# Cross attention of layer 0: the own scores' exponential one task later on ScalarE, every copy of turned rows in the own tasks by ScalarE, and the filling shared anew

## The chip, the cores and the metric

The kernel runs on one core of a Trainium2 chip. The metric is the device time of one execution in microseconds; lower is better. All arithmetic is in f32.

## The reference, cut to what matters

Two decoder layers run over `x` of shape (8, 112, 512): attention, cross attention and a feed-forward block each. The change lies in the cross attention of layer 0. It computes attention over the sequence's own rows and, beside it, attention over a context of 375 rows, with shared projections:

```python
q = split_heads(hidden_states @ Wq, q_len)           # 32 heads of 16
k = split_heads(hidden_states @ Wk, q_len)
v = split_heads(hidden_states @ Wv, q_len)
q = q * cos + _rotate_half(q) * sin
k = k * cos + _rotate_half(k) * sin
scores = jnp.einsum('bhqd,bhkd->bhqk', q, k) * inv_sqrt_d
scores = jnp.maximum(scores + attention_mask, jnp.finfo(scores.dtype).min)
w = jax.nn.softmax(scores.astype(jnp.float32), axis=-1)
attn_output = jnp.einsum('bhqk,bhkd->bhqd', w, v)
a_k = split_heads(adapter @ Wk, adapter_len)         # adapter: the context, 375 rows
a_v = split_heads(adapter @ Wv, adapter_len)
a_scores = jnp.einsum('bhqd,bhkd->bhqk', q, a_k) * inv_sqrt_d
a_scores = jnp.tanh(gate) * jax.nn.softmax(a_scores, axis=-1)
attn_output = attn_output + jnp.einsum('bhqk,bhkd->bhqd', a_scores, a_v)
return attn_output.transpose(0, 2, 1, 3).reshape(bsz, q_len, hid) @ Wo
```

## The kernel before

One list of steps, made by `build_order`, is walked by every engine; each engine issues its own part of each step and skips steps in which it has none. So the order on every queue is the order of that list, and engines wait for one another by semaphores alone.

In the cross attention of layer 0 (8 batches) the 32 heads of a batch are taken in 4 groups of 8 heads. Each group is three **tasks** (`TASKS`): `own` (the 8 heads' scores over the sequence, 112x896), then context task 0 and context task 1 (4 heads each, 112x375 a head). There are 96 tasks. All three kinds put their scores into PSUM banks 0 to 3, so the scores of one task wait until the task before has read them out. A task's later parts lie one to three tasks behind (`attendx`):

- task n, scores: `xs` (own, L1032) or `xc` (context, L1043) on TensorE.
- task n, own: VectorE adds the mask and so empties the banks (`xm` 0, L1420), takes the maximum (L1426), clamps it (L1432) and subtracts it (L1434). ScalarE then takes one exponential over 112x896 (`xe`, L1900), which sums of `xm` 3 (L1429) and the transposes of task n+2 read.
- task n, context: VectorE takes the maxima out of PSUM (`cm`, L1442, two heads each), ScalarE four exponentials out of PSUM with their sums (`ce`, L1908), which empty the banks.
- task n+2: the exponentials are turned by TensorE: `xt` (own, L1052, two banks) or `xct` (context, L1059, three banks, 12 transposes). Each turned bank is copied to SBUF as 112x448 or 125x448: `turned_by` gives the engine, ScalarE for 0 (L1915, L1921) and VectorE for 1 (L1449, L1455). Before the change the third of three `xct` banks is VectorE's.
- task n+3: products with the values, `xv` (L1069) and `xcv` (L1079), into bank 7; `xu` (L1927) copies it out on ScalarE.

So the own task of group c turns context task 0 of group c-1, context task 0 turns context task 1 of group c-1, and context task 1 turns the own scores of group c. Once per batch, `xd` (reciprocals, L1462, L1464), `xr` (L1087, L1932), `xb` (L1095, L1470 to L1475) and `xw` (the output projection, L1104, L1387) follow in the tasks 2 to 5 of the next batch.

The steps that take PSUM here beside the scores (`xct`, `xt`, `xb`, `xw` and all filling) share three banks, `LOW` = 4, 5, 6, in the order of the list (`place`).

Between a task's `head` (exponentials, maxima, transposes) and its `tail` (the value products) stands **filling**, work for later that needs no task: projections of the next batch's context (`ck`, L1011, copied by L1888 on ScalarE and L1404 on VectorE; `cv`, L1020, copied by L1895 and L1411), of its queries and keys (`pj`, L988; `rt`, L995), and `vx` (L1003). `cross` shares it out: a batch's whole cost times the task's share in `GAP` is a task's due, its own steps are taken off, and filling is laid in until the due is used up. Batch 7, the last, has no projection to fill with, only transposes for the experts (L908).

Of the kernel before, what the change touches and what calls it, by code (L numbers as in the profile page):

```python
# [176 lines left out]
def cost(step):  # L177
    return COST.get(step[0], 0.0)
# [60 lines left out]


TASKS = [(b, c, kind) for b in range(NBATCH) for c in range(4) for kind in ("own", 0, 1)]
GAP = {"own": 3.0, 0: 5.5, 1: 5.5}


def shifts(n):

    if n >= len(TASKS):
        return []
    b, c, kind = TASKS[n]
    return [("xm", b, c, k) for k in range(3)] if kind == "own" else [("cm", b, c, kind, r) for r in (0, 2)]  # L250


def attendx():

    gaps = []
    for n in range(len(TASKS) + 3):
        turns, tail, mine = [], [], shifts(n)
        if 2 <= n < len(TASKS) + 2:  # L260
            b, c, kind = TASKS[n - 2]
            turns = [("xt", b, c, par) for par in range(2)] if kind == "own" else [("xct", b, c, kind, t) for t in range(3)]
        head = []
        for k in range(3):
            head += mine[k:k + 1] + turns[k:k + 1]
        if n < len(TASKS):
            b, c, kind = TASKS[n]
            head += [("xe", b, c)] if kind == "own" else [("ce", b, c, kind, r) for r in (0, 2)]
        if 2 <= n < len(TASKS) + 2 and TASKS[n - 2][2] == "own":
            tail.append(("xm", *TASKS[n - 2][:2], 3))  # L270
        if n >= 3:
            b, c, kind = TASKS[n - 3]
            tail += [("xv", b, c, par) for par in range(2)] if kind == "own" else [("xcv", b, c, kind, t) for t in range(3)]
            if kind == 1:
                tail.append(("xu", b, c))
        gaps.append((head, tail))
    for b in range(NBATCH):
        for k, step in ((2, ("xd", b)), (3, ("xr", b)), (4, ("xb", b)), (5, ("xw", b))):
            head, tail = gaps[min(12 * (b + 1) + k, len(gaps) - 1)]
            if step[0] in ("xd", "xr") or 12 * (b + 1) + k >= len(gaps):  # L280
                tail.append(step)
            else:
                head.append(step)
            if step[0] == "xw":
                tail.append(("stats", 2, b))
    return gaps
# [10 lines left out]
def cross():  # L297

    out, gaps = [], attendx()
    for b in range(NBATCH):  # L300
        fill = context(b + 1) + [("load", "ct", b + 2)] * (b + 2 < NBATCH) + [("vx", b + 1)] if b + 1 < NBATCH else [("load", "front", j) for j in (1, 2, 0)]
# [9 lines left out]
        whole = sum(cost(s) for s in fill + late) + sum(cost(s) for n in mine for part in gaps[n] for s in part)  # L311
        unit = whole / sum(GAP[TASKS[n][2]] for n in mine)
        due = 0.0
        for n in mine:
            if n == mine[2]:
                fill += late
            out.append(("xs" if TASKS[n][2] == "own" else "xc", *TASKS[n][:2], *TASKS[n][2:][:TASKS[n][2] != "own"]))
            due += unit * GAP[TASKS[n][2]]
            head, tail = gaps[n]
# [193 lines left out]
def psum_use(step, late):  # L513
# [36 lines left out]
    if k in ("xt", "xct"):  # L550
        return LOW, 1, [(("even_out", "odd_out")[turned_by(step)], step)]
# [37 lines left out]
def turned_by(step):  # L589

    k, b, c, par = step[:4]
    return par if k == "xt" else int(step[4] == 2)


def chunk_starts(l):
# [29 lines left out]
def program(nc, a, out):  # L625
    with ExitStack() as ctx:
# [268 lines left out]
        def tensor(e, w):  # L895
# [166 lines left out]
            def xv(b, c, par):  # L1062
                if par == 0 and (b or c):
                    w.wait_ge(*at("ou", (b, c - 1) if c else (b - 1, 3)))
                w.wait_ge(*at("vx", (b,)))
                w.wait_ge(*out_of(("xt", b, c, par), turned_by(("xt", b, c, par))))
                for r in range(4):
                    h = (8 * c + 2 * r + par) * 32
                    o = e.matmul(PS[32 * r:32 * r + 32, 7, bcol(2 * (c % 2))], VX[b % 2][0:S, h:h + 32],  # L1069
                                 px_of["xt", b, c, par][0:S, bcol(r)], start=par == 0, stop=par == 1)  # L1070
                o.then_inc(*up("values", ("xv", b, c, par)))

            def xcv(b, c, par, t_):
                s = ("xct", b, c, par, t_)
                w.wait_ge(*out_of(s, turned_by(s)))
                w.wait_ge(*out_of(("cv", b, t_), t_))
                for r in range(4):
                    h = (8 * c + 2 * r + par) * 32
                    o = e.matmul(PS[32 * r:32 * r + 32, 7, bcol(2 * (c % 2) + 1)], Vc[b % 2][0:KC, t_, h:h + 32],  # L1079
                                 px_of[s][0:KC, bcol(r)], start=(par, t_) == (0, 0), stop=(par, t_) == (1, 2))  # L1080
                o.then_inc(*up("values", ("xcv", b, c, par, t_)))
# [1333 lines left out]
```

## Time and profile before

| | us |
|---|---|
| median of 3 runs | 1978.99 |
| lowest, highest | 1974.83, 1980.17 |
| the profiled execution, its own time | 1975.63 |
| its span, first to last instruction | 1973.7 |
| busy in the span: TensorE (PE) | 1848.8 (94%) |
| busy: VectorE (DVE) | 1027.8 (52%) |
| busy: ScalarE (ACT) | 591.2 (30%) |
| busy: GpSimd (POOL) | 392.7 (20%) |
| mean granted TensorE clock | 0.966 |

The busy share is a mean over stages. The tasks of the change run from 436 us, where the first `xs` starts, to about 1018 us, and the chain of work that ended last passes through TensorE for 74% of the whole span. The granted clock is a share of 2.4 GHz; 0.5 is 1.2 GHz.

### The profile page before, as it was taken

The page shows a single profiled execution, that of the slowest core. Times are in us where ns is not written, and L with a number is a line of the kernel's source. Part 1 is how long each engine was busy: PE and PEld are TensorE (multiplying, and loading weights), DVE is VectorE, ACT ScalarE, POOL GpSimd, SP SyncE. Part 2 cuts the span into 40 slices and gives each one's busy share as a digit, 9 for nine tenths or more (in the row PEclk, how much of TensorE's full clock was granted, in tenths as well). Part 3 has the DMA queues.
Part 4 walks back from the last instruction along what each step waited for, and adds up shares of the span by engine and source line. Part 5 has one row for each costly group of instructions (what it writes and reads, how often), then busy time and mean ns, then how long its engine had stood idle before and what let it go on. Part 6 is the DMA issues. An engine that isn't in the chain of part 4 may idle for free.

```text
span 1973.7 us, 29165 instructions
## 1 busy us (share of the span) xinstructions
PE 1848.8 (94%) x11802; PEld 1214.3 (62%) x11802; DVE 1027.8 (52%) x1892; ACT 591.2 (30%) x1899; POOL 392.7 (20%) x456
## 2 busy tenths in 40 slices
PE   6899999999999999999888999997899999999798
PEld 5766666645665665666554888876576674444344
DVE  3665556426566655566653111115644454464699
ACT  0223223315454444555640011100312213232411
POOL 2432222410110110110003000005121120000588
PEclk9999999999999999999888999998899999999899
DMA  9000002000000000000205888874000011543011
GB/s 377 21 1 1 1 1 102 1 30 17 1 17 16 2 17 1 17 17 2 108 27 225 303 334 333 341 270 142 1 1 1 1 72 77 224 166 117 0 38 38
DMA packets 30965, 170.70 MB, mean 86 GB/s; under 512 B 3848, under 2 KB 3848, under 8 KB 17168
## 3 DMA queue, kind: packets, MB, share of 16 engines
q1 hardware_dynamic: 28272, 161.50, 21.9%
q0 software_dynamic: 2560, 7.34, 1.2%
q8 instruction: 94, 1.54, 0.3%
q14 instruction: 39, 0.32, 0.1%
HBM read 155.98 MB, written 16.52 MB: 87 GB/s over the span
## 4 chain that ended last, share of the span: by engine, by line
PE 74%; DVE 12%; issue 4%; POOL 4%; ACT 3%; DMA 2%; SPq 0%; POOLq 0%; DVEq 0%; ACTq 0%
PE PS L1143 8%; PE PS L980 6%; PE PS L931 6%; PE PS L1223 6%; PE PS L1183 5%; PE PS L1020 5%; PE PS L1011 4%; PE PS L1152 4%; PE PS L1256 3%; PE PS L988 2%; PE PS L1043 2%; PE PS L1059 2%; PE PS L1079 2%; PE PS L1052 1%; PE PS L1214 1%
## 5 line engine op out<-in xcount | busy, mean ns | idle before, releaser
L2046 POOL TENSOR_TENSOR rstd<-veps,mhalf 112x1 f32<-112x1 f32 (+1 forms) x76 | 57.5, 758 | 623.3 <-DVE veps L1316 609.0
L1143 PEld LDWEIGHTS PS<-R,W 128*128 128x128 f32 x1344 | 155.9, 195 | 11.9 <-issue 11.9
L1442 DVE TENSOR_REDUCE nmx<-PS 112x2 f32<-112x750 f32 x128 | 114.0, 932 | 91.0 <-PE PS L1043 90.9
L1143 PE MATMUL PS<-R,W 128*128 128x128 f32 x1344 | 156.3, 278 | 2.2 <-DVE R L1613 2.2
L1908 ACT ACTIVATE R<-PS,nmx 112x375 f32<-112x375 f32 x256 | 142.8, 574 | 1.3 <-DVE nmx L1442 1.3
L1387 DVE TENSOR_TENSOR x<-x,PS 112x512 f32<-112x512 f32 x40 | 27.5, 687 | 194.6 <-PE PS L1223 90.5
L931 PE MATMUL PS<-xT,W 128*128 128x224 f32 x640 | 125.3, 356 | 0.0
L931 PEld LDWEIGHTS PS<-xT,W 128*128 128x128 f32 x640 | 122.3, 192 | 4.9 <-issue 4.4
L1059 PE MATMUL PS<-cst,R 112*125 112x112 f32 x768 | 107.8, 286 | 13.0 <-DVE R L1455 9.2
L1620 DVE TENSOR_TENSOR R<-R,PS 128x512 f32<-128x512 f32 x21 | 14.4, 687 | 201.9 <-PE PS L1143 201.9
L1256 PE MATMUL PS<-W 128*128 128x512 f32 x256 | 118.0, 604 | 0.0
L1059 PEld LDWEIGHTS PS<-cst,R 112*125 112x125 f32 x768 | 92.0, 191 | 37.8 <-issue 15.6
L1223 PE MATMUL PS<-W,R 128*112 128x512 f32 x256 | 113.2, 595 | 0.8 <-DVE R L1672 0.8
L980 PE MATMUL PS<-W,R 128*112 128x512 f32 x256 | 113.7, 597 | 0.0
L2064 POOL TENSOR_TENSOR R<-R 128x224 f32<-128x224 f32 x80 | 52.8, 660 | 271.4 <-DVE R L1337 271.4
L1287 PE MATMUL PS<-W,xT 128*128 128x512 f32 x224 | 102.4, 601 | 1.9 <-ACT xT L1849 1.9
L1860 ACT ACTIVATE R<-PS,small 112x112 f32<-112x112 f32 x256 | 87.0, 388 | 47.1 <-DVE small L1355 47.1
L1183 PEld LDWEIGHTS PS<-xT,W 128*128 128x128 f32 x512 | 96.9, 190 | 1.6 <-issue 1.6
L1183 PE MATMUL PS<-xT,W 128*128 128x224 f32 x512 | 97.5, 352 | 0.0
L1020 PE MATMUL PS<-W 128*125 128x512 f32 x192 | 92.4, 628 | 1.3 <-ACT W L1921 0.6
L1011 PE MATMUL PS<-W 128*128 128x375 f32 x256 | 87.0, 489 | 4.5 <-DMA W<-in_ctxT 3.9
L980 PEld LDWEIGHTS PS<-W,R 128*112 128x112 f32 x256 | 44.1, 177 | 67.6 <-issue 67.6
(292 smaller groups left out, 3310.9 us busy)
## 6 DMA issues: line engine op xcount, KB each, us to landing
W<-in_we SPq DMA_DIRECT2D x63, 1024.0 KB, 7.4
W<-in_entwT SPq DMA_DIRECT2D x8, 1024.0 KB, 7.0
W<-in_entpw SPq DMA_DIRECT2D x8, 1024.0 KB, 8.7
W<-in_ctxT SPq DMA_DIRECT2D x8, 750.0 KB, 4.2
R<-in_ctxT SPq DMA_DIRECT2D x8, 750.0 KB, 8.1
R<-in_ctx SPq DMA_DIRECT2D x8, 750.0 KB
xs_rows<-in_x SPq DMA_DIRECT2D x3, 1792.0 KB, 39.1
R<-xs_rows SPq DMA_DIRECT2D x21, 256.0 KB, 7.8
```

The source lines that it names most:

```text
L931: o = e.matmul(PS[:, m, ab * UT:(ab + 1) * UT], lw, xT[:, k, tok], start=k == 0, stop=k == 3)
L980: o = e.matmul(PS[0:S, m, :], OT[:, n % 2, c, :], Wo[:, g * 8 + c, :], start=c == 0, stop=c == 7)
L1011: o = e.matmul(PS[:, m, 0:SC], Wx[1][:, k, c * 128:(c + 1) * 128], CT[:, k, :], start=k == 0, stop=k == 3)
L1020: o = e.matmul(PS[0:KC, m, :], CT[:, k, t * KC:(t + 1) * KC], Wx[2][:, k, :], start=k == 0, stop=k == 3)
L1059: t = e.transpose(PS[0:KC, m, bcol(r)], p_of(b, c, par)[0:S, r, t_ * KC:(t_ + 1) * KC], ident[0:S, 0:S])
L1143: o = e.matmul(PS[:, m, c * 128:(c + 1) * 128], gate_up(j % 3, k, off + c * 128), BT[:, j % 2, k, :], start=k == 0, stop=k == 3)
L1183: o = e.matmul(PS[:, m, ab * UT:(ab + 1) * UT], Wlq[c // 2][:, c % 2, k, ab * 128:ab * 128 + 128], xT[:, k, tok], start=k == 0, stop=k == 3)
L1223: o = e.matmul(PS[0:S, m, :], LOT[:, n % 2, c, :], Wlo[2 * g + c // 4][:, c % 4, :], start=c == 0, stop=c == 7)
L1256: o = e.matmul(PS[:, m, :], W[:, wt, kk * D + m * 128:kk * D + (m + 1) * 128], W[:, pw, kk * D:(kk + 1) * D], start=k in starts, stop=k + ...
L1287: o = e.matmul(PS[:, m, :], xT[:, k, tcol(t)], wk[:, k, :], start=k == 0, stop=k == 3)
L1442: e.tensor_reduce(nmx[0:S, par, r:r + 2], PS[0:S, r:r + 2, 0:SC], AX.X, ALU.max, negate=True).then_inc(*up("cmax", (b, c, par, r)))
L1908: e.activation(p_of(b, c, par)[0:S, r, :], PS[0:S, r, 0:SC], ACT.Exp, bias=nmx[0:S, par, r:r + 1], accum_out=sums[0:S, b % 2, n:n + 1]).th ...
```

## The change

Three things, all in the order of the steps. `xe`, the exponential of the own scores, moves out of the own task into context task 0 behind it, where it stands behind the ScalarE copies of turned rows and ahead of the four `ce`. `turned_by` gives the third `xct` bank to VectorE only in context task 0 (`par` 1, third bank); in the own task (`par` 0) all three are now ScalarE's. And `GAP` gives context task 0 a share of 6.5 and context task 1 of 5.0, where both had 5.5.

```diff
-GAP = {"own": 3.0, 0: 5.5, 1: 5.5}
+GAP = {"own": 3.0, 0: 6.5, 1: 5.0}
...
         if n < len(TASKS):
             b, c, kind = TASKS[n]
-            head += [("xe", b, c)] if kind == "own" else [("ce", b, c, kind, r) for r in (0, 2)]
+            if kind == 0:
+                head.append(("xe", b, c))
+            head += [("ce", b, c, kind, r) for r in (0, 2)] if kind != "own" else []
...
 def turned_by(step):
     k, b, c, par = step[:4]
-    return par if k == "xt" else int(step[4] == 2)
+    return par if k == "xt" else int(step[3:] == (1, 2))
```

The lines of the program below the change lie two lower in the changed kernel: L1900 is L1902 there. No instruction is added or dropped; 32 copies of 125x448 change engine. Queues of GpSimd and of the DMA issues (SP) keep their order of instructions.

On ScalarE, batch 4, own task of group 1 and context task 0 behind it, before. L1921 are copies of turned rows, L1900 is `xe`, L1932 is `xr`'s copy, L1908 are `ce`, L1895 a copy of `cv`:

```order
L1927 ACTIVATE W<-PS 128x224
L1921 ACTIVATE row<-PS 125x448 x2
L1900 ACTIVATE R<-R 112x896
L1932 ACTIVATE rT<-PS 32x224
L1921 ACTIVATE R<-PS 125x448 x2
L1908 ACTIVATE R,sums<-PS,nmx 112x375 x4
L1895 ACTIVATE W<-PS 125x16x2x16
```

The same place now:

```order
L1929 ACTIVATE W<-PS 128x224
L1923 ACTIVATE row<-PS 125x448 x2
L1923 ACTIVATE R<-PS 125x448
L1934 ACTIVATE rT<-PS 32x224
L1923 ACTIVATE R<-PS 125x448 x2
L1902 ACTIVATE R<-R 112x896
L1910 ACTIVATE R,sums<-PS,nmx 112x375 x4
L1897 ACTIVATE W<-PS 125x16x2x16
```

The own task has a third copy, and the exponential of 112x896 stands behind the next task's two copies.

On VectorE, the same two tasks before. L1420 to L1434 are `xm`, L1455 the copies of turned rows, L1442 `cm`, L1470 `xb`:

```order
L1420 TENSOR_TENSOR R<-PS,R 112x896
L1426 TENSOR_REDUCE sx<-R 112x8
L1432 TENSOR_SCALAR sx<-sx 112x8
L1434 SCALAR_TENSOR_TENSOR R<-R,sx 112x896
L1455 COPY R<-PS 125x448
L1442 TENSOR_REDUCE nmx<-PS 112x2 x2
L1455 COPY W<-PS 125x448
L1470 TENSOR_TENSOR R<-W,PS 128x448
```

And now:

```order
L1422 TENSOR_TENSOR R<-PS,R 112x896
L1428 TENSOR_REDUCE sx<-R 112x8
L1434 TENSOR_SCALAR sx<-sx 112x8
L1436 SCALAR_TENSOR_TENSOR R<-R,sx 112x896
L1444 TENSOR_REDUCE nmx<-PS 112x2 x2
L1457 COPY W<-PS 125x448
L1472 TENSOR_TENSOR R<-W,PS 128x448
```

The first of the two copies is gone from between the own scores' subtraction and the next task's maxima.

On TensorE, batch 5, context task 0 of group 1 up to the own task of group 2, before (L1043 `xc`, L1059 `xct`, L1095 `xb`, L1079 `xcv`, L1052 `xt`, L1104 `xw`, L1032 `xs`, L1020 the filling `cv`):

```order
L1043 MATMUL PS<-W,R 112x375 x4
L1059 MATMUL PS<-cst,R 125x112 x12
L1095 MATMUL PS<-rT,cst 128x112 x8
L1079 MATMUL PS<-R,W 32x112 x12
...
L1104 MATMUL PS<-W,R 112x512 x4
...
L1032 MATMUL PS<-R 112x112 x8
L1059 MATMUL PS<-cst,R 125x112 x12
L1020 MATMUL PS<-W 125x512 x4
```

And now:

```order
L1045 MATMUL PS<-W,R 112x375 x4
L1061 MATMUL PS<-cst,R 125x112 x12
L1097 MATMUL PS<-rT,cst 128x112 x8
L1022 MATMUL PS<-W 125x512 x4
L1081 MATMUL PS<-R,W 32x112 x12
...
L1106 MATMUL PS<-W,R 112x512 x4
...
L1034 MATMUL PS<-R 112x112 x8
L1061 MATMUL PS<-cst,R 125x112 x12
```

One `cv` has moved from the own task into the context task 0 that had no filling but `xb`. In all, ten steps of filling move between neighbouring tasks: into context task 0 go `ck` of batches 2, 4 and 5 (first quarter) and `ck` 7 (last quarter), `cv` 6 and `vx` 6 from own tasks, `cv` 3, one `pj` and one `ck` 7 from context tasks 1, and one `rt`. Of batch 7, where there is nothing to move, all stands as before.

## Rows read from the trace of the kernel before

**Rows 1.** Windows: busy us (count) of PE, PEld, DVE, ACT, POOL, clock, DMA share, GB/s

```profile
425.00:1020.00 595.00, 563.13 (x5037) 363.07 (x5036) 365.13 (x518) 300.53 (x826) 54.63 (x74) 0.96 0.06 20
```

**Rows 2.** Waits of TensorE, 425 to 1020 us: total us, times, longest

```profile
PE PS L1059 <- DVE R L1455: 9.2, 13, 1.2
...
PE PS L1059 <- DVE row L1455: 3.1, 5, 1.2
...
PE PS L1095 <- ACT R L1921: 1.3, 5, 0.3
...
PE PS L1020 <- ACT W L1921: 0.6, 3, 0.2
...
PE PS L1020 <- ACT R L1921: 0.4, 2, 0.2
PE PS L1020 <- ACT row L1921: 0.4, 2, 0.2
```

**Rows 3.** Waits of TensorE in batch 7 alone, 945 to 1020 us

```profile
PE PS L1043 <- ACT R L1908: 5.2, 3, 2.2
...
PE PS L1059 <- DVE R L1455: 1.2, 2, 1.0
...
PE PS L1059 <- DVE row L1455: 0.3, 1, 0.3
```

**Rows 4.** Timeline, batch 4, own task of group 1: start, us, instruction, [wait]

```profile
755.75 1.56 PE L1059 MATMUL PS<-cst,R 112*125 112x112 f32 x12
...
758.89 0.69 PE L1059 MATMUL PS<-cst,R 112*125 112x112 f32 x4
760.83 1.37 PE L1059 MATMUL PS<-cst,R 112*125 112x112 f32 x8 [1.25 <-DVE R L1455]
762.45 3.72 PE L1095 MATMUL PS<-rT,cst 32*128 32x112 f32 x16 [0.25 <-ACT R L1921]
766.10 5.19 PE L1020 MATMUL PS<-W 128*125 128x512 f32 x8
...
759.15 1.09 DVE L1434 SCALAR_TENSOR_TENSOR R<-R,sx 112x896 f32<-112x896 f32 x1
760.16 0.62 DVE L1455 COPY R<-PS 125x448 f32<-125x448 f32 x1
...
756.48 0.98 ACT L1921 ACTIVATE row<-PS 125x448 f32<-125x448 f32 x2 [0.82 <-PE PS L1059]
760.27 0.95 ACT L1900 ACTIVATE R<-R 112x896 f32<-112x896 f32 x1 [2.81 <-DVE R L1434]
761.13 0.33 ACT L1932 ACTIVATE rT<-PS 32x224 f32<-32x224 f32 x1
```

**Rows 5.** Windows at the `xb` places of batches 4, 2 and 5 (columns as in rows 1)

```profile
761.00:768.00 7.00, 6.75 (x27) 5.19 (x28) 3.86 (x6) 3.49 (x12) 0.00 (x0) 0.59 0.00 1
...
611.00:614.00 3.00, 3.00 (x39) 1.89 (x39) 2.15 (x4) 0.19 (x3) 0.00 (x0) 0.69 0.00 0
...
838.00:843.00 5.00, 4.71 (x64) 3.82 (x56) 3.56 (x5) 3.28 (x11) 0.00 (x0) 1.00 0.00 0
```

**Rows 6.** Timeline, the same forms at full clock, batches 5 and 2

```profile
840.31 2.00 PE L1095 MATMUL PS<-rT,cst 32*128 32x112 f32 x16 [0.29 <-ACT row L1921]
...
618.44 3.60 PE L1020 MATMUL PS<-W 128*125 128x512 f32 x8
```

**Rows 7.** Timeline, batch 2: group 2's context task 0 ends, task 1 begins

```profile
630.32 0.60 ACT L1908 ACTIVATE R<-PS,nmx 112x375 f32<-112x375 f32 x1
...
632.75 0.90 PE L1043 MATMUL PS<-W,R 32*112 32x375 f32 x8
```

**Rows 8.** Timeline, batch 7: group 3's context task 0 and the wait behind it

```profile
1004.79 0.95 ACT L1900 ACTIVATE R<-R 112x896 f32<-112x896 f32 x1 [1.11 <-DVE R L1434]
...
1006.74 0.54 ACT L1921 ACTIVATE R<-PS 125x448 f32<-125x448 f32 x1
...
1009.64 0.90 PE L1043 MATMUL PS<-W,R 32*112 32x375 f32 x8 [1.79 <-ACT R L1908]
```

## The prediction

> **What bounds the kernel now.** I read the page's busy shares and chain first (TensorE, 74% of the chain), then the windows of the stage. From 425 to 1020 us TensorE is busy 563.1 of 595 us while VectorE has 365 and ScalarE 301 [rows 1]. So TensorE is the bound here, and a change of order can win only what TensorE waits, 31.9 us at most, and what its clock loses: 0.96 of full speed is the stage's mean.
>
> Then the waits of TensorE in that stage [rows 2]. The largest is L1059, the transposes `xct`, for L1455, a VectorE copy of a turned bank: 9.2 us in 13 waits and 3.1 us in 5, together 12.3 us in 18. Behind most of them a short wait for the first ScalarE copy follows where the next filling wants its bank: L1020 for L1921, 0.6 + 0.4 + 0.4 = 1.4 us in 7.
>
> The timeline shows why [rows 4]. The own task's 12 transposes are done at 757.3 us (755.75 + 1.56), and its third bank lies ready for VectorE. But VectorE has the chain of `xm` ahead of the copy: the subtraction L1434 runs from 759.15, and only at 760.16 does L1455 start. There are three banks for these steps, so the next context task's transposes stop after the first bank (758.89) and go on at 760.83, after 1.25 us. ScalarE meanwhile waits: L1900 sits idle 2.81 us for the same subtraction, and the ready copies of context task 0 queue behind it.
>
> **Part 1, the third copy goes to ScalarE (`turned_by`).** ScalarE copies two such tiles in 0.98 us from 756.48 [rows 4] and one in 0.54 [rows 8], so each further one adds 0.44. The third would end near 757.9 at this place, 2.9 us before 760.83, in time in which ScalarE had nothing to do. The 32 copies thus cost ScalarE 32 x 0.44 = 14 us of its idle time, cost the path nothing, and give VectorE back 32 x 0.62 = 20 us, which it does not need except in batch 7. If the cover went (ScalarE late in the own task), each copy would cost up to 0.44 us.
>
> What goes is the 12.3 us. In batch 7 three of the 18 waits, 1.2 + 0.3 = 1.5 us, stand ahead of a wait for `ce`, which is late next (5.2 us in 3) [rows 3]; I don't count them. That leaves 12.3 - 1.5 = **10.8 us**. The 1.4 us at L1020 go too, since the first bank's copy then has the time of two more banks' transposes: **1.4 us**. The waits of L1095 for L1921 (1.3 us in 5 in rows 2, 0.25 in rows 4) need the last ScalarE copy of context task 0, which still comes just behind its transposes, and stay. Bounds for this part: 12.3 + 1.4 = 13.7 if batch 7 gives its share too, and half, 6, if other waits take the place of every second one.
>
> Here a rule of the Trainium skill speaks against the change. By "TensorEngine Tiling (Array Packing)", section PSUM Bottleneck, one should use both ScalarE and VectorE to empty PSUM. The rows show the reason failing here: two engines help only if the second is free, and VectorE starts its copy 3.7 us after ScalarE started its first [rows 4]. By the rule each own task would lose the overlap of one copy, 0.44 us, 14 us in all; by the rows it loses none of it. I go by the rows; the case in which ScalarE is the bound is a rival below.
>
> **Part 2, `xe` one task later.** `xe` has 0.86 us of ScalarE's time at this place (760.27 to 761.13), between a wait and the copies of context task 0 [rows 4]. In its new place the copies go first, in the time in which ScalarE waited for the subtraction, and `xe` comes when it is ready. Where context task 0 starts early (own task without filling), copies plus `xe` end when they did before, so `ce` starts no later: cost 0. Its readers, `xm` 3 and the transposes `xt`, stand in context task 1, a task later: no wait. Where context task 0 starts late (own task with filling, or TensorE at 1.2 GHz), `xe` had run in idle time and now stands on ScalarE between the copies and `ce`, 0.86 us. Whether that costs depends on the slack between the last `ce` and the next scores. With filling in context task 0 it is large: the last `ce` begins at 630.32 and ends by 631.0, the scores start at 632.75, 1.7 us later [rows 7]. The places with least slack were those whose context task 0 had no filling, and part 3 fills them. Only batch 7 is left, four groups. In group 3 `xe` ran at 1004.79, before the copies (1006.74), and TensorE then waited 1.79 us for `ce` [rows 8]: **+0.9 us** there. In another group of batch 7 VectorE, rid of its copy, reaches the maxima earlier: about -0.8 from the 1.0 us wait in rows 3. Sum **0**, bounds -2 and +3.4 (four groups at 0.86).
>
> **Part 3, the filling.** Ten steps move to a neighbour; TensorE's work is the same. A context task 1 that loses its filling has `xw` or one `ck` left, so its own `ce` stay hidden. Cost 0; if that cover is too thin, the next `xs` waits for `ce`, as it does in batch 7.
>
> **Part 4, the clock.** At 761 us the granted clock falls right after the wait of 1.25 us: its mean is 0.59 from 761 to 768, mostly the 1.2 GHz level [rows 5]. What that costs is in the rows: L1095 took 3.72 against 2.00 us at full speed, L1020 took 5.19 against 3.60 [rows 4, 6], and 0.2 us more in L1059: 1.7 + 1.6 + 0.2 = 3.5 us. There are three such places with a wait of 1.2 us (batches 1, 3 and 4, group 1, all with `xb`), each followed by a slow stretch. At the `xb` of batch 5, where the only wait is 0.29 us, the clock stays at 1.00 [rows 5, 6]. Batch 2, again with no long wait there, fell briefly all the same: 0.69 from 611 to 614 [rows 5]. So taking the wait away should help at most of the three, not surely at each: I take two of three, 2 x 3.5 = **7 us**, bounds 0 and 3 x 3.5 and 1.5 for batch 2's (3 us at half speed), 12 us.
>
> **Sum**, against the profiled execution (1975.6 us, 3.4 below the median of the runs, within their spread): 10.8 + 1.4 + 0 + 7 = 19.2, so 1956.4. A new median may lie above its like by up to 3.4; I add half, 1.7, and say **1958 us**.
>
> **The rivals.**
> - *Only the waits go, the clock stays as it is* (the falls belong to the small matmuls around `xb`, not to the wait): 1975.6 - 12.2 + 1.7 = 1965. For it: batch 2 fell without a long wait. Against: three of three with the wait, one of several without. Chance 0.25, beside 0.47 for my forecast; with all slow stretches gone it would be 1953.
> - *The waits move*: TensorE comes sooner and waits for `ce`, for the copies behind them or for VectorE's filling copies, so that half of part 1 is left and no clock: 1979.0 - 6.1, about 1972. For it: batch 7 shows what is late next [rows 3]. Against: 1.7 us of slack in filled tasks. Chance 0.15.
> - *ScalarE becomes the bound* (slower): in context task 0 copies, `xe` and four `ce` now stand in one row, and if the last `ce` ends after TensorE has done its part, every group pays 0.86 us, 32 x 0.86 = 27.5. Less 12.2 that is +15, 1991 to 1994. It decides where the slack behind `ce` is under 0.86 us; rows 7 has 1.7, batch 7 has none. It breaks even at 14 of 32 groups. Chance 0.05.
> - *Nothing to see*: gain and price cancel, or the waits removed were ahead of others everywhere: 1973 to 1985. Chance 0.08.
>
> **How the numbers follow.** A measurement of this kernel tells about 0.3% from no change, 6 us; faster means under 1973. My forecast (0.47) and the clock rival (0.25) lie under it, the half case (0.15) mostly: 0.85 faster. Same takes its rest and the null case: 0.10. Slower: 0.05. The range goes from all slow stretches gone with some of batch 7, 1948, to the half case, 1972.
>
> **What would show it.** Right: no waits of `xct` (now L1061) for VectorE's L1457 in the own-to-context transitions; the third own copy on ScalarE within 2 us of the first; ScalarE's idle time ahead of L1902 near zero instead of 2 to 3 us; the stage, first `xs` to last `xcv`, shorter by 12 to 24 us, all else the same; granted clock in the stage up from 0.96. Wrong: new waits of `xc` (L1045) for `ce` (L1910) outside batch 7, or of `xs` (L1034) for it in batches 1 to 6; or waits gone and the clock as low as before, which points to the second case.

## The result, and the profile after

| us | before | changed |
|---|---|---|
| median | 1976.93 (4 runs, 1974.83 to 1980.17) | 1944.93 (4 runs, 1944.2 to 1950.63) |
| profiled execution, its span | 1973.7 | 1942.9 |
| mean granted clock over the span | 0.966 | 0.975 |

The ratio is 0.9846, with a 95% interval of 0.9823 to 0.987: 32 us less between the medians, 30.8 us between the spans. (The median before was 1978.99 when it had three runs; the fourth took 1974.87.) The forecast said 1958, 19 us below the profiled execution and 21 below the median of then, in a range down to 1948. The direction was right, the size too small by about a third, and the measured time lies 3 us below the range.

The page of the changed kernel, part 1: VectorE loses 18 us and ScalarE gains 13, as 32 copies changed engine. TensorE does the same 11802 matmuls in 21 us less.

```profile
PE 1827.4 (94%) x11802; PEld 1202.3 (62%) x11802; DVE 1009.9 (52%) x1860; ACT 604.6 (31%) x1931; POOL 392.4 (20%) x456
```

The waits of TensorE in the stage of the tasks, 425 to 1000 us of the changed kernel, in the columns of [rows 2]:

```profile
PE PS L1045 <- ACT R L1910: 8.3, 4, 2.7
...
PE PS L1045 <- DVE R L1422: 3.3, 7, 0.5
PE PS L910 <- DVE R L1326: 1.6, 1, 1.6
PE PS L1097 <- ACT R L1923: 1.4, 5, 0.3
```

All 18 waits of the transposes for VectorE's copy (12.3 us in [rows 2]) are gone, and so are the seven of L1020 for ScalarE's copy behind them (1.4 us). L1097 for L1923 stayed, as forecast. The waits for `ce`, L1910, grew from 5.2 us in 3 to 8.3 in 4, all in batch 7. Those for the mask's addition, L1422, grew too; before they were:

```profile
PE PS L1043 <- DVE R L1420: 1.9, 4, 0.5
```

The timeline of the place of [rows 4], batch 4, own task of group 1 with context task 0 behind it, in the changed kernel:

```profile
736.30 1.56 PE L1061 MATMUL PS<-cst,R 112*125 112x112 f32 x12
...
739.44 1.56 PE L1061 MATMUL PS<-cst,R 112*125 112x112 f32 x12
741.29 2.00 PE L1097 MATMUL PS<-rT,cst 32*128 32x112 f32 x16 [0.29 <-ACT R L1923]
743.22 3.70 PE L1022 MATMUL PS<-W 128*125 128x512 f32 x8
```

ScalarE there:

```profile
737.02 0.98 ACT L1923 ACTIVATE row<-PS 125x448 f32<-125x448 f32 x2 [0.82 <-PE PS L1061]
737.90 0.54 ACT L1923 ACTIVATE R<-PS 125x448 f32<-125x448 f32 x1
...
740.16 0.98 ACT L1923 ACTIVATE R<-PS 125x448 f32<-125x448 f32 x2 [1.10 <-PE PS L1061]
741.04 0.94 ACT L1902 ACTIVATE R<-R 112x896 f32<-112x896 f32 x1
741.88 0.57 ACT L1910 ACTIVATE R<-PS,nmx 112x375 f32<-112x375 f32 x1
```

The 12 transposes run in one piece; the third own copy follows the first two at once; the next task's copies go when their banks are turned and not when the own exponential is done; the exponential L1902 follows them without waiting, and `ce` starts 0.84 us behind it. L1097 takes 2.00 us and L1022 3.70, where they took 3.72 and 5.19: the clock did not fall.

The windows of the whole stage, first `xs` to the last products of the tasks, to a whole us (the last products end at 1018.7 before and at 988.6 after), columns as in [rows 1]. Before:

```profile
436.00:1018.00 582.00, 550.13 (x4989) 357.35 (x4992) 363.08 (x515) 299.58 (x824) 48.48 (x71) 0.96 0.06 20
```

After:

```profile
436.00:988.00 552.00, 529.67 (x4990) 347.53 (x4994) 345.20 (x483) 312.97 (x856) 48.44 (x71) 0.98 0.06 21
```

TensorE's busy time in these windows falls by 20.5 us and its idle time by 9.5. Before and after, the traces show the granted clock at 1.0 or 0.5 only. The two-digit means of such long windows are coarse, so I add up windows of 10 us over the same stretches: 51 us at 1.2 GHz before, 24 after. At the lower level the same matmuls take about twice as long (3.72 us against 2.00 for `xb`'s), so half of a stretch is lost: an estimate of 27 / 2 = 13.6 of the 31 us came from the clock.

### The profile page after: what moved, and what is told of

It reads as the page before. It is cut to its first block, busy times and chain, and to the rows that moved or that the text cites. A ratio compares the mean times of both kernels' runs of the same rounds, so it can differ in the third digit from the quotient of the medians.

```text
span 1942.9 us, 29167 instructions
## 1 busy us (share of the span) xinstructions
PE 1827.4 (94%) x11802; PEld 1202.3 (62%) x11802; DVE 1009.9 (52%) x1860; ACT 604.6 (31%) x1931; POOL 392.4 (20%) x456
## 4 chain that ended last, share of the span: by engine, by line
PE 78%; DVE 9%; issue 4%; POOL 4%; ACT 2%; DMA 2%; SPq 0%; POOLq 0%; DVEq 0%; ACTq 0%
PE PS L1145 8%; PE PS L1225 6%; PE PS L982 6%; PE PS L933 6%; PE PS L1185 5%; PE PS L1022 4%; PE PS L1013 4%; PE PS L1061 4%; PE PS L1154 4%; PE PS L1258 3%; PE PS L1045 3%; PE PS L990 2%; PE PS L1081 2%; PE PS L1216 1%; PE PS L1054 1%
## 5 line engine op out<-in xcount | busy, mean ns | idle before, releaser
L1145 PEld LDWEIGHTS PS<-R,W 128*128 128x128 f32 x1344 | 156.0, 195 | 11.9 <-issue 11.9
L1910 ACT ACTIVATE R<-PS,nmx 112x375 f32<-112x375 f32 x256 | 142.9, 573 | 0.8 <-DVE nmx L1444 0.8
L1061 PEld LDWEIGHTS PS<-cst,R 112*125 112x125 f32 x768 | 89.8, 190 | 20.8 <-issue 16.8
L1061 PE MATMUL PS<-cst,R 112*125 112x112 f32 x768 | 101.3, 282 | 0.0
L1022 PE MATMUL PS<-W 128*125 128x512 f32 x192 | 86.8, 597 | 0.0
```

The lines of the kernel that those rows point to most:

```text
L1022: o = e.matmul(PS[0:KC, m, :], CT[:, k, t * KC:(t + 1) * KC], Wx[2][:, k, :], start=k == 0, stop=k == 3)
L1061: t = e.transpose(PS[0:KC, m, bcol(r)], p_of(b, c, par)[0:S, r, t_ * KC:(t_ + 1) * KC], ident[0:S, 0:S])
L1145: o = e.matmul(PS[:, m, c * 128:(c + 1) * 128], gate_up(j % 3, k, off + c * 128), BT[:, j % 2, k, :], start=k == 0, stop=k == 3)
L1910: e.activation(p_of(b, c, par)[0:S, r, :], PS[0:S, r, 0:SC], ACT.Exp, bias=nmx[0:S, par, r:r + 1], accum_out=sums[0:S, b % 2, n:n + 1]).th ...
```

## The experiments

Unless said otherwise each was timed beside the kernel before, whose median was 1975.4 to 1976.6 in these comparisons.

### The parts by themselves: e1, e2, e3, e4

e1, the third own copy to ScalarE, nothing else:

```diff
-    return par if k == "xt" else int(step[4] == 2)
+    return par if k == "xt" else int(step[3:] == (1, 2))
```

> The kernel before with turned_by alone changed: the own task's third copy goes to ScalarE, the own exponential and the filling stay. The prediction's step has this part carry the gain: the 12 us of waits of the transposes L1059 for VectorE's copy gone, and the clock at the three places with them, about 1956 to 1965 us. The rival reading now: the exponential still stands on ScalarE ahead of the next task's copies, and what follows the transposes (filling, or the 16 matmuls L1095) waits for those copies until the same moment, so the wait only moves from L1059 for VectorE to L1020 and L1095 for L1921: 0 to 5 us gained, 1972 to 1977 us, and L1095 waits over 1 us at the places of batches 1, 3 and 4.

Measured: 1978.2 us, ratio 1.0015 (1.0005 to 1.0025). Nothing is gained; it is 2.7 us slower. The waits of TensorE, e1, 425 to 1020 us:

```profile
PE PS L1059 <- ACT rT L1932: 5.9, 5, 1.5
...
PE PS L1020 <- ACT W L1921: 3.9, 3, 1.5
PE PS L1020 <- ACT R L1921: 2.5, 2, 1.5
PE PS L1020 <- ACT row L1921: 2.0, 2, 1.2
```

And the timeline at the place of [rows 4], e1, TensorE and then ScalarE:

```profile
757.98 1.12 PE L1059 MATMUL PS<-cst,R 112*125 112x112 f32 x8
760.60 0.78 PE L1059 MATMUL PS<-cst,R 112*125 112x112 f32 x4 [1.49 <-ACT rT L1932]
761.54 3.72 PE L1095 MATMUL PS<-rT,cst 32*128 32x112 f32 x16 [0.16 <-ACT R L1921]
...
759.36 0.95 ACT L1900 ACTIVATE R<-R 112x896 f32<-112x896 f32 x1 [2.37 <-DVE R L1434]
760.22 0.33 ACT L1932 ACTIVATE rT<-PS 32x224 f32<-32x224 f32 x1
760.45 0.94 ACT L1921 ACTIVATE R<-PS 125x448 f32<-125x448 f32 x2
```

The third own copy is early, and no transpose waits for VectorE. But the exponential L1900 still waits 2.37 us for the subtraction with `xr`'s copy L1932 and the next copies L1921 behind it. The waits for VectorE have become waits for ScalarE of the same length and more, and the clock falls as before (3.72 for L1095). From the start of the interrupted transposes to that of L1095 it is 3.56 us in both kernels (757.98 to 761.54 here, 758.89 to 762.45 in [rows 4]): with the first wait gone, TensorE gets no further. The rival reading held; where I expected L1095 to wait over a microsecond, it was the last transposes ahead of it, whose bank the late L1932 frees.

e2, the own exponential alone moved into context task 0:

> The kernel before with the own exponential alone moved into context task 0. VectorE's third copy stays between the subtraction and the maxima, so the waits L1059 <- L1455 (12.3 us in 18) stay as they are. Only the short waits for L1921 behind them can go (about 0.19 us each, some 7 to 11 of them, and what a restart costs beside the wait). Prediction's working: nothing gained by this part alone, 1977 us. The rival reading: 3 to 6 us gained, 1971 to 1974.

Measured: 1974.38 us, ratio 0.9973 (0.995 to 0.9995): 1 us less by the medians, 5 by the ratio. The two differ because the ten runs spread widely: six took 1973.65 to 1977.49 us, one 1969.16, and three 1961.29 to 1964.27, with a mean granted clock of 0.972 to 0.974 where the kernel before has 0.965 to 0.969. So this kernel, waits and all, sometimes keeps the clock. Its profile is of a run of 1973.65: the waits for VectorE's copy stand there (9.4 us in 13 and 3.1 in 5, 425 to 1020 us); those for ScalarE's copy behind them are gone.

e3, the shares of filling alone:

> The kernel before with the shares of filling alone changed. Prediction's working: same work, other places, 0. The rival that the filling brings a part of the 32 us: then over 6 us here. An own task without filling gets the wait for VectorE's copy that it hid before (five more places at 0.3 to 1.0 us), so it could lose 2 to 6 us instead, more where the clock falls too: 1977 to 1983.

Measured: 1985.95 us, ratio 1.005 (1.0037 to 1.0063), 10 us slower. The waits of TensorE, e3:

```profile
PE PS L1059 <- DVE R L1455: 11.0, 16, 1.2
PE PS L1059 <- DVE row L1455: 5.5, 8, 1.2
```

Six own tasks that had hidden VectorE's late copy behind a projection lost it and wait too: 24 waits and 16.5 us, for 18 and 12.3 in [rows 2]. The waits for the mask's addition grew as well, to 3.3 us in 7 from 1.9 in 4. These 5.6 us, and the price of 9 more stops that e6 shows below (0.24 us each), make about 8 of the 10.

e4, both moves, the shares as before:

> Both moves, filling as before. If the two moves work only together, this has nearly all of the gain: 1945 to 1952 us. What the new shares add is then the rest: context tasks 0 without filling behind an own task with filling (three places) have the exponential ahead of the last ce and wait about 0.4 to 0.9 us each, 2 us in all. If the filling carries much, this stays over 1958.

Measured: 1944.64 us, ratio 0.9845 (0.9819 to 0.9872). That is the whole gain. So the two moves, which alone give nothing and 1 to 5 us, give over 30 together: each takes away one of two waits that ended at nearly the same moment. The new shares add nothing to them that these measurements can tell; in the lists they trade waits: e4 has 9.2 us in 7 for `ce` and 1.9 in 4 for the mask's addition, the changed kernel 8.3 in 4 and 3.3 in 7.

### Where the third copy counts, and what the clock does: e5, e6, e9

e5 is the changed kernel with VectorE's copy back in the own tasks that turn group 0, beside `xr` and `xb`:

```diff
-    return par if k == "xt" else int(step[3:] == (1, 2))
+    return par if k == "xt" else int(step[4] == 2 and not (par == 0 and c != 0))
```

> The changed kernel, except that VectorE keeps the third copy in the own tasks that turn group 0 (those of group 1, where xr and xb of the batch before stand beside). So the wait of 1.2 us comes back in batches 1, 3 and 4, and smaller ones in 6 and 7; batches 2 and 5 hide it behind filling. Theory that the falls of the clock hang on the wait: the granted clock falls again right behind each of the three, each costs about 4.9 us (as the changed kernel gained there) and the time is 1958 to 1962. Rival, that the falls belonged to the small matmuls of xb or to chance: only the waits return, 3 x 1.5 and the two small ones, 1949 to 1951 us, with the clock at full speed at two or three of the places.

Measured: 1963.45 us, ratio 0.9931 (0.9915 to 0.9948), 18.5 us above the changed kernel. Its waits for VectorE's copy are six, 5.4 us. The rest is mostly the clock: it fell again behind all three waits of 1.25 us, and further low stretches came in batches 6 and 7, where two more of the waits are. The theory held; 18.5 is a little over its range (13 to 17 us).

e6 is the complement, VectorE's copy back in all other own tasks:

```diff
-    return par if k == "xt" else int(step[3:] == (1, 2))
+    return par if k == "xt" else int(step[4] == 2 and not (par == 0 and c == 0 and b))
```

> The complement: VectorE keeps the third copy in the own tasks that turn groups 1 to 3, ScalarE has it where xb stands. 12 or 13 waits L1061 for L1457 of 0.3 to 1.0 us come back (about 7 us in the list of waits with those of batch 7). If a wait costs what its row says, 1951 to 1952 us. Theory that it costs 0.2 to 0.3 us more than its row, because the matmuls' pipeline has to fill again (places with 0.49 us of waits in two rows gained 0.98): 1953 to 1956. The clock stays up at the three xb places under both.

Measured: 1963.49 us, ratio 0.9934 (0.9917 to 0.995), 18.5 us above the changed kernel, outside both expectations. One reason is that there were more waits than I had counted. Its list:

```profile
PE PS L1061 <- DVE R L1457: 8.1, 13, 1.0
...
PE PS L1061 <- DVE row L1457: 3.8, 6, 1.0
```

These are 19 waits and 11.9 us, since the new shares leave more own tasks unfilled. The other is what a wait costs beside its row. Batch 0, own tasks of groups 1 and 2 and what follows, TensorE in e6:

```profile
459.29 1.12 PE L1061 MATMUL PS<-cst,R 112*125 112x112 f32 x8
461.23 0.69 PE L1061 MATMUL PS<-cst,R 112*125 112x112 f32 x4 [0.82 <-DVE row L1457]
461.75 3.61 PE L1022 MATMUL PS<-W 128*125 128x512 f32 x8
...
475.34 1.12 PE L1061 MATMUL PS<-cst,R 112*125 112x112 f32 x8
477.02 0.69 PE L1061 MATMUL PS<-cst,R 112*125 112x112 f32 x4 [0.56 <-DVE R L1457]
477.55 3.61 PE L1022 MATMUL PS<-W 128*125 128x512 f32 x8
```

The first of these two places in the changed kernel, with no wait:

```profile
458.98 1.56 PE L1061 MATMUL PS<-cst,R 112*125 112x112 f32 x12
460.38 3.62 PE L1022 MATMUL PS<-W 128*125 128x512 f32 x8
```

From the first transpose to the first `cv` it is 1.40 us without a wait, 2.46 with a wait of 0.82 and 2.21 with one of 0.56. So a wait costs its row and **0.24 us** more. The busy times around a stop overlap less: 1.12 and 0.69 make 1.81 us where twelve in one piece take 1.56. With that, e6's 19 waits are 11.9 + 19 x 0.24 = 16.5 us, and one more low stretch, at the `xb` of batch 1 (clock 0.72 over 6 us, so 1.7 us lost), makes it 18.2, near the 18.5 measured.

e9 is the kernel before with one edit, VectorE's reciprocals one task earlier, so that the wait of 1.25 us shrinks:

```diff
-        for k, step in ((2, ("xd", b)), (3, ("xr", b)), (4, ("xb", b)), (5, ("xw", b))):
+        for k, step in ((1, ("xd", b)), (3, ("xr", b)), (4, ("xb", b)), (5, ("xw", b))):
```

> The kernel before with one edit: the reciprocals xd (L1462, L1464, 0.73 us of VectorE together) stand one task earlier, so that at the xb places VectorE's chain and its third copy end about 0.7 us sooner. The wait L1059 for L1455 there shrinks from 1.25 to about 0.5 us in batches 1, 3 and 4; nothing else of the change is in. If the clock falls because of the length of that wait, it may stay up at some of the three and the time falls by 2 (waits) to 12 us: 1964 to 1974. If any restart there is enough, or if the fall belongs to the place, it falls at all three again and only 2 us are gained.

Measured: 1969.19 us, ratio 0.9965 (0.9952 to 0.9979). The three waits are 0.55 us now. Windows of 6 us behind L1095 in batches 1 and 4, columns as in [rows 1]:

```profile
530.10:536.10 6.00, 6.00 (x19) 4.27 (x20) 2.41 (x5) 2.05 (x8) 0.00 (x0) 0.53 0.00 0
759.18:765.18 6.00, 6.00 (x44) 3.69 (x48) 2.41 (x5) 2.38 (x9) 0.00 (x0) 1.00 0.01 3
```

The clock fell in batches 1 and 3 and stayed up in batch 4: 3 x 0.7 us of waits, 3.4 for the slow stretch and 1.7 for batch 2's, which did not come either, make 7.2 us, near the 6.2 measured.

All profiles together show what hangs on the wait. The first three rows of the table have the mean granted clock in the 6 us from the start of the 16 matmuls of `xb`, at the places of batches 1, 3 and 4; the last two have it in the 6 us behind waits that stand elsewhere, with no `xb` behind them (batch 7, where other waits stand close by, is left out; L1095's own wait of up to 0.3 us is not counted as one):

| wait of the transposes ahead of `xb`, or elsewhere | kernels | places | clock fell at |
|---|---|---|---|
| 1.24 us or more | before, e1, e2, e3, e5 | 15 | 15 (mean 0.50 to 0.72) |
| 0.55 us | e9 | 3 | 2 (0.52, 0.53) |
| none | changed, e4, e6, e7, e8, e10, e11, e12 | 24 | 5 (0.72 each) |
| 1.03 us, transposes, batches 1 to 6, no `xb` behind | before, e2, e3, e6, e9 | 21 | 3 (0.72, 0.72, 0.73) |
| 1.47 us, `cv`, batches 1, 3 and 4, no `xb` behind | e1 | 3 | 0 |

Two windows of the table's kind, TensorE at the place of batch 4 in e1, with the wait, and of batch 1 in e5, which got it back:

```profile
761.54:767.54 6.00, 6.00 (x19) 4.60 (x20) 2.37 (x4) 2.05 (x8) 0.00 (x0) 0.50 0.00 0
```

```profile
526.73:532.73 6.00, 6.00 (x20) 4.63 (x20) 2.49 (x4) 2.86 (x9) 0.00 (x0) 0.50 0.00 0
```

And behind a wait of 1.03 us in batch 4 of e6, with no `xb`:

```profile
769.97:775.97 6.00, 6.00 (x48) 3.08 (x49) 3.08 (x5) 2.73 (x9) 0.00 (x0) 1.00 0.00 0
```

At the `xb` places the matmuls are the same in all kernels, so there the wait decides: 15 of 15 profiled places with it, 5 of 24 without. The stretches are longer with it, too: all five falls without a wait show 0.72, and eleven of the fifteen with it lie lower. But the wait alone is not enough. Elsewhere waits of 1.03 and 1.47 us were followed by a fall at 3 of 24 places, while at `xb` even 0.55 us was enough at two of three. So the fall goes with the wait and with the work of the place together. Nor is it certain: each kernel has one profile, and three of e2's ten runs, none of them profiled, took 12 us less with a clock that stayed higher.

### Beyond the change: e7, e8, e10, e11, e12

e7 puts the own exponential behind the four `ce`:

```diff
-            if kind == 0:
-                head.append(("xe", b, c))
             head += [("ce", b, c, kind, r) for r in (0, 2)] if kind != "own" else []
+            if kind == 0:
+                head.append(("xe", b, c))
```

> The changed kernel with the own exponential behind the four ce of context task 0 instead of ahead of them. In batch 7 TensorE waits 8.3 us for ce in 4 waits; each of the three behind a context task 0 should shrink by 0.86. The transposes of the own scores come 0.8 us after the next scores and may wait for the exponential now, by 0.2 us at most. Elsewhere the slack hides both places. Theory: 2 to 3 us gained, 1941 to 1943. Rival, that ce's delay was the maxima's and not the exponential's: 0, 1945.

Measured: 1946.23 us, ratio 0.9846 (0.9829 to 0.9862). No gain: the list of waits for `ce` shrinks from 8.3 us in 4 to 6.4 in 3, but other waits come in batch 7 (L1061 for L1841, 0.7 us; L910 for L1326, 2.1 for 1.6). And in its profile the clock fell at the `xb` of batches 1 and 2 (0.72 over 6 us each), which costs 3.4 us that the changed kernel's profile did not pay. Neither the theory (a gain of 2 to 3 us) nor its rival is settled by the time.

e8 takes VectorE's sums and statistics out of the way as well:

```diff
         if 2 <= n < len(TASKS) + 2 and TASKS[n - 2][2] == "own":
-            tail.append(("xm", *TASKS[n - 2][:2], 3))
+            head.append(("xm", *TASKS[n - 2][:2], 3))
...
             if step[0] == "xw":
-                tail.append(("stats", 2, b))
+                later = gaps[12 * (b + 1) + 6][1] if 12 * (b + 1) + 6 < len(gaps) else tail
+                later.append(("stats", 2, b))
```

> As e7, and two pieces of VectorE's work out of the way of the own scores: the sums of xm 3 right behind the maxima of context task 1 instead of behind its filling, and the statistics behind xw one task later. The waits of xc L1045 for the mask's addition L1422 (3.3 us in 7) should go: with what a restart adds, 4 to 5 us less than e7, 1937 to 1940 us. Rival: the addition to x of xw still stands ahead there (0.7 us), so the waits shrink and don't go: 1 to 2 us.

Measured: 1941.5 us, ratio 0.9821 (0.9804 to 0.9837). The waits for the mask's addition (L1422, 3.3 us in 7) are gone from its list. That is 4.7 us below e7, as expected, from a higher start, so above the range of 1937 to 1940.

e10 is e8 with the old shares, e11 the changed kernel again beside it:

> As e8 (exponential behind ce, VectorE's sums and statistics out of the way), but with the old shares of filling. e4 and the changed kernel agree, so the shares brought nothing while the exponential stood ahead of ce; behind ce the three unfilled context tasks 0 lose their last reason to wait. Theory: no difference to e8, 1939 to 1943 us. If the new shares help now, 1944 or more.

> The changed kernel once more, beside e10 on the same chip, since e8's gain over it (3.4 us) was measured in another job: 1944 to 1947 us, 3 to 5 us above e10.

Measured: e10 1945.2 us (0.9855, 0.9838 to 0.9872), e11 1945.43 us (0.9851, 0.9838 to 0.9865). The repeat agrees with the first result. e10 came out above e8, so I ran e8 again:

> e8's kernel once more with five rounds, since e8 (1941.5) lay 3.9 us under the changed kernel's repeat (1945.4) and e10, which differs from it in the shares of filling alone, did not (1945.2). If e8 is really ahead of the changed kernel by the 3.3 us of waits that it takes away: 1940 to 1942.5, ratio to before 0.981 to 0.984. If e8's four runs were lucky with the clock and the gain is given back, 1944 to 1946, ratio 0.984 to 0.986.

Measured: 1941.78 us, ratio 0.9829 (0.9816 to 0.9843). The two medians lie 3.2 to 3.9 us below the two of the changed kernel, as its 3.3 us of waits ask; the intervals still touch, so it is likely ahead, by 0.2%, and not shown to be. Why e10's median does not follow is open. Nothing in its profile speaks for the new shares: from the first `xs` to the last products it has 549.4 us, and e8 and e12 have 550.8; what it is longer by lies outside the stage of the tasks. Its runs spread from 1943.3 to 1949.8, with a clock of 0.974 down to 0.970.

## Why the prediction was right and wrong

Two terms of the sum were too small: part 1's waits (12.2 us put down, 16.2 found) and part 4's clock (7 put down, 13.4 found). And part 1's account of which move earns its term was wrong.

**What bounds the kernel, and where the gain comes from: right.** From the first `xs` to the last products it is 582.5 us before and 552.7 after, so 29.8 of the 30.8 us lie there (12 to 24 were forecast), in the waits of TensorE that end on VectorE's and ScalarE's copies and in the clock behind them. The transposes' waits for VectorE went, those of L1095 stayed.

**Part 1, `turned_by`: right in what goes, wrong in what carries it, and mis-sized.** The step gave the 12.2 us to the copy on ScalarE, and put `xe`'s move at 0 in part 2. e1 shows that the copy alone gives nothing. The next wait in line, for ScalarE's copies behind the exponential, ended so close behind the first that TensorE, freed of the first, waits to nearly the same moment. The rows had it as the 0.2 to 0.25 us that TensorE waited again, and I priced those at their length. Moved together the two parts work, so the sum was not hurt. The size was: a wait costs its row plus 0.24 us, and the 10.8 us stood in 15 places, which is 3.6 us more. Eleven short waits for ScalarE's copy stand behind the long ones: the seven at L1020 that I counted, and four at L1011 and L988, 0.8 us together, that I left out. Over batches 0 to 6 the changed kernel gained 27.9 us (from the starts of `xs` in the two timelines: 951.25 and 923.03, less 0.3 that they differ at the start). About 10.3 of it are the three clock stretches and 1.4 batch 2's, which leaves 16.2 for a term of **12.2**. The split between waits and clock is an estimate.

**Part 2, `xe` one task later: right that it costs next to nothing, wrong that nothing is gained by it** (it carries part 1's gain as much as the copy does). In group 3 of batch 7 the forecast was 0.9 us more waiting for `ce`; [rows 8] has 1.79 and the changed kernel has 2.63:

```profile
979.32 0.90 PE L1045 MATMUL PS<-W,R 32*112 32x375 f32 x8 [2.63 <-ACT R L1910]
```

In group 2 it was 0.8 less; from own task to own task that group went from 15.22 to 14.37 us. No new wait for `ce` appeared outside batch 7. But batch 7 as a whole was not 0, it gained 1.8 us: group 1 gained 2.1, where the clock had been low before, at L1043 and L1052, and was not now.

**Part 3, the filling: 0, as forecast, but not for the reason given.** By themselves the new shares cost 10 us (e3), for the greater part because filling in an own task hid VectorE's copy. With the copy on ScalarE that price is gone, and so is any gain (e4).

**Part 4, the clock: the mechanism right, the size too small.** I took two of the three slow stretches, 7 us. All three went, and batch 2's and, on balance, some of batch 7's with them: 10.3 + 1.4 + 1.7 = **13.4 us**, the last from group 1, near the 13.6 of the windows. The rival that the falls belong to the place and not to the wait is refuted in its strong form by 15 of 15 against 5 of 24; that the place has a part in it is shown by the waits elsewhere, 3 of 24. I treated the three as a lottery from one counter-example, batch 2, with bounds of 0 to 12; the three waits of 1.25 with a fall behind each were the stronger evidence. Some luck is in the size all the same: batch 2's stretch is absent in the profiles of e1, e2, e3, e5 and e9 too, which keep the waits, and e7, which has none, has one there. And 0.2 of the 3.5 us for a stretch was misread: the eight transposes took 1.37 us in batch 7 too, where the clock was at 1.00, so that is not the clock's:

```profile
973.04 1.37 PE L1059 MATMUL PS<-cst,R 112*125 112x112 f32 x8 [0.21 <-DVE R L1455]
```

**The base.** I added 1.7 us since the profiled execution lay below the median. The new median (1944.93) lies 0.2 above its profiled execution (1944.75), so nearly all of this went the wrong way.

Together: 16.2 for 12.2, 13.4 for 7, 0.1 for 0 in batch 7 beside the clock, and 1.0 outside the stage, which I put at nothing, make 30.7 for 19.2. The range's lower end, 1948, allowed for all slow stretches and had no term for what a stop costs.

The rule of the Trainium skill that I weighed, use both ScalarE and VectorE to empty PSUM ("TensorEngine Tiling (Array Packing)", PSUM Bottleneck), would have had the changed kernel 14 us behind in its own tasks. The trace goes against it here: the third copy on ScalarE starts at 737.90, 0.88 us after the first, where VectorE's started 3.7 us after it [rows 4], and giving some of these copies back to VectorE cost 18.5 us in e5 and as much in e6.

## What to carry to other kernels

When two engines both hand over late at one place, price the removal of the first wait at the distance to the second, and look for the second wait just behind in the timeline: a short wait that follows a long one may be a long one half hidden. Add to each removed wait of TensorE what stopping and starting costs (here 0.24 us per stop), and the slow stretch that follows, where the trace shows one each time at such a place. And try parts of such a change together before dropping them: here the parts by themselves were 3 us slower, 1 to 5 faster and 10 slower, and the whole 32 faster.

## What the runs showed that I had not expected

A wait of TensorE of 1.24 us or more ahead of the small matmuls of `xb` was followed by the 1.2 GHz level at 15 of 15 places, one of 0.55 us at 2 of 3, none at 5 of 24. Waits of 1.03 us and more elsewhere were followed by it at 3 of 24, so the wait does it only with the work of that place. Before the fall TensorE had been busy but for that wait and a short one behind it, with matmuls of 32 rows among the work (scores, `xb`). In the kernel before a stretch cost about 3.4 us, nearly three times the wait ahead of it.
